# Two heads on the two partition halves for the first 64 queries of the diagonal blocks in a fused attention and channel-mix kernel

## What is computed

```python
raw = jnp.einsum('bhid,bhjd->bhij', q, k)
scores = sips_alpha[0] * jnp.tanh(raw / sips_beta[0])
scores = scores + lam * hamming[:, None, :, :]       # hamming = soft_bits @ soft_bits.T / 2
scores = scores + lat                                # hexc_i Mh hexc_j, per head
scores = jnp.where(causal[None, None], scores, -jnp.inf)
attn = jax.nn.softmax(scores, axis=-1)
out = jnp.einsum('bhij,bhjd->bhid', attn, v)
...
x = _layernorm(x + attention(x))
x = _layernorm(x + r * (k_act @ W_v.T))              # r = sigmoid(xr W_r), k_act = relu(xk W_k) ** 2
```

## Time and profile before

| | us |
|---|---|
| median of 3 runs | 400.71 |
| lowest, highest | 400.51, 401.08 |
| the profiled execution | 402.91 |
| its span in the trace | 401.2 |

### The profile page before, as it was taken

How to read it: one execution, slowest core, us unless ns; L and a number is a source line. 1 busy time by engine, 2 the same in 40 slices (tenths; PEclk the granted TensorE clock), 3 DMA queues, 4 the chain that set the end, 5 groups by cost and what they waited for, 6 DMA issues and landing times.

```text
span 401.2 us, 9042 instructions
## 1 busy us (share of the span) xinstructions
PE 361.6 (90%) x3045; PEld 209.1 (52%) x3045; DVE 333.0 (83%) x536; ACT 327.9 (82%) x367; POOL 229.8 (57%) x367
## 2 busy tenths in 40 slices
PE   7788878489999999999999999999989998989983
PEld 7473433134665565655564556455634564445572
DVE  4878979348999999989999999999978977797654
ACT  1216899538998999899999999899989998999811
POOL 4516557314578648765777567956684537344542
PEclk9999999859999999999999999999999999999998
DMA  4264786787613576357544763475337630100000
GB/s 127 72 192 144 233 235 177 205 236 174 155 59 116 159 196 176 100 157 189 154 139 128 203 158 116 146 204 159 117 116 209 174 95 2 54 26 3 2 28 26
DMA packets 37809, 53.76 MB, mean 134 GB/s; under 512 B 3523, under 2 KB 35267, under 8 KB 36191
## 3 DMA queue, kind: packets, MB, share of 16 engines
q1 hardware_dynamic: 32909, 50.83, 45.9%
q10 hardware_dynamic: 4865, 2.49, 2.5%
HBM read 38.69 MB, written 14.61 MB: 133 GB/s over the span
## 4 chain that ended last, share of the span: by engine, by line
PE 54%; DVE 12%; ACT 10%; issue 7%; DMA 6%; SPq 6%; POOL 4%; POOLq 0%; DVEq 0%; ACTq 0%
PE raw L521 25%; PE side_bank L521 13%; PE sums L521 12%; DMA i_stack<-hamming_i 5%; ACT probs L829 4%; DVE probs L1073 4%; ACT probs L834 4%; PE side_bank L613 3%; SPq L387 2%; POOL parts L975 2%; POOL res L1003 1%; DVE bn L1158 1%; DMA probs<-in_L_attn_hex_w 1%; SPq L403 1%; ACT k_act L846 1%
## 5 line engine op out<-in xcount | busy, mean ns | idle before, releaser
L1073 DVE SCALAR_TENSOR_TENSOR probs<-probs,scal,raw 128x1024 f32<-128x1024 f32 x160 | 202.3, 1273 | 35.6 <-PE raw L521 35.0
L829 ACT ACTIVATE probs<-raw 128x1024 f32<-128x1024 f32 x160 | 164.4, 1028 | 33.0 <-PE raw L521 30.6
L834 ACT ACTIVATE probs<-probs 128x1024 f32<-128x1024 f32 x160 | 169.8, 1063 | 0.3 <-DVE probs L1073 0.3
L962 POOL TENSOR_SCALAR_AFFINE_SELECT probs<-probs 128x256 f32<-128x256 f32 (+1 forms) x224 | 97.2, 450 | 114.0 <-ACT probs L834 113.6
L521 PE MATMUL raw<-i_stack,j_stack 111*128 111x384 bf16 (+3 forms) x512 | 97.8, 303 | 11.7 <-DMA i_stack<-hamming_i 7.8
L521 PE MATMUL raw<-q_stack,k_stack 72*128 72x384 bf16 (+3 forms) x512 | 97.8, 303 | 9.6 <-DVE probs L1073 7.5
L521 PE MATMUL sums<-probs,values 128*32 128x256 f32 (+2 forms) x1280 | 82.4, 384 | 0.4 <-POOL probs L962 0.4
L521 PEld LDWEIGHTS raw<-q_stack,k_stack 72*128 72x128 bf16 x512 | 42.4, 98 | 58.8 <-DVE probs L1073 27.4
L521 PEld LDWEIGHTS raw<-i_stack,j_stack 111*128 111x128 bf16 x512 | 41.4, 98 | 55.8 <-issue 22.6
L521 PEld LDWEIGHTS sums<-probs,values 128*32 128x32 f32 x1280 | 33.8, 109 | 30.2 <-issue 20.0
L975 POOL TENSOR_TENSOR parts<-whole,parts 128x512 bf16<-128x512 f32 x30 | 35.6, 1195 | 3.8 <-DVE parts L1112 3.1
(11 more groups left out here) (154 smaller groups left out, 347.8 us busy)
## 6 DMA issues: line engine op xcount, KB each, us to landing
q_stack<-q_rows SPq DMA_DIRECT2D x21, 384.0 KB
k_stack<-k_rows SPq DMA_DIRECT2D x21, 384.0 KB
i_stack<-lattice_i SPq DMA_DIRECT2D x21, 288.0 KB
i_stack<-hamming_i SPq DMA_DIRECT2D x21, 288.0 KB
q_rows<-parts SPq DMA_DIRECT2D x8, 384.0 KB, 4.3
k_rows<-parts SPq DMA_DIRECT2D x8, 384.0 KB, 2.6
k_rows<-parts SPq DMA_DIRECT2D x8, 256.0 KB, 2.9
x_res<-in_L_attn_x SPq DMA_DIRECT2D x8, 256.0 KB, 3.0
```

Of the source, the lines that this page charges most:

```text
L829: nc.scalar.activation(pair_probs(t), raw[:, t % PSUM_PAIRS, :].rearrange("p (u i) -> p u i", u=2), ACT.Tanh).then_inc(tanh_done, 1)
L834: nc.scalar.activation(pair_probs(t), pair_probs(t), ACT.Exp).then_inc(exp_done, 1)
L962: last = nc.gpsimd.affine_select(out=v, in_=v, compare_op=ALU.is_ge, fill=0.0, base=0, pattern=[[0, v.shape[1]], [1, P]], channel_multipli ...
L1073: v.scalar_tensor_tensor(out=o, in0=o, scalar=scal[:, 2:3], in1=raw[:, t % PSUM_PAIRS, :].rearrange("p (u i) -> p u i", u=2), op0=ALU.mult ...
```

## The change

Each diagonal block of 128 x 128 is cut at query 64. Its first 64 queries see only the block's first 64 keys. These 64 x 64 squares leave the ordinary pairs: the product of key block jb now starts at query 128 jb + 64 and has 448, 320, 192 or 64 columns, so a quad takes four pairs in place of five. The squares of 8 heads (four key blocks each) are put into one *square pair*, the first four heads on partitions 0 to 63, the other four on 64 to 127. A half batch (8 heads) has 8 ordinary pairs and one square pair, and a batch 18 pairs.

With it come these edits. The square pair's scores are 32 products of 64 x 64, its biases 8 of 64 x 256; a new operand `square_values` holds the two halves' values one above the other, 0 elsewhere, filled by two more copies of VectorE in `values_in`. The ordinary masks are two selects of 2 x 64 columns. The square mask is a product with `triangle`, one GpSimd instruction over 1024 elements. The `mid` parts of batches from the loop on are made by GpSimd, by subtraction, not by VectorE's cast. `PAIR_BUFFERS` is 9. All step tables are new for 18 steps. GpSimd fills the new constants in the set-up.

```diff
-PAIR_BUFFERS = 10
+PAIR_BUFFERS = 9
-VALUES_STEPS = [7, 9, 9, 9, 9, 13, 13, 14, 14, 14, 19, 19, 19, 20, 20, 23, 23, 25, 25, 25]
+VALUES_STEPS = [8, 8, 8, 8, 10, 10, 14, 14, 14, 17, 17, 17, 17, 20, 20, 23, 23, 23]
...
+            k, j = divmod(t, HALF_PAIRS)
+            quad, p = 2 * k + j // 4, j % 4
+            heads = [4 * quad + 2 * (p % 2) + u for u in range(2)]
             if p < 2:
...
+                return [[(h, 3, 0), (h, 0, SQUARE)] for h in heads]
+            return [[(h, 2, 0), (h, 1, P + SQUARE)] for h in heads]
...
+                if is_square(t):
+                    for jb in range(JB):
+                        for r in range(4):
+                            for s in range(2):
+                                first_key = square_heads(t, s)[r] * T + jb * P
+                                at = 4 * SQUARE * jb + SQUARE * r
+                                last = mm(raw[SQUARE * s:SQUARE * (s + 1), t % PSUM_PAIRS, at:at + SQUARE],
+                                          k_stack[par][:, first_key:first_key + SQUARE],
+                                          q_stack[par][:, first_key:first_key + SQUARE])
...
+                if is_square(t):
+                    for jb in range(JB):
+                        for s in range(2):
+                            heads = square_heads(t, s)
+                            at = 4 * SQUARE * jb
+                            queries = i_stack[par][:, heads[0] * T:(heads[3] + 1) * T] \
+                                .rearrange("p (r i) -> p r i", r=4)[:, :, jb * P:jb * P + SQUARE]
+                            last = mm(raw[SQUARE * s:SQUARE * (s + 1), t % PSUM_PAIRS, at:at + 4 * SQUARE],
+                                      j_stack[par][:, jb * P:jb * P + SQUARE], queries)
...
+                if is_square(t):
+                    squares = pair_probs(t).rearrange("p u i -> p (u i)")
+                    for jb in range(JB):
+                        for r in range(4):
+                            at = 4 * SQUARE * jb + SQUARE * r
+                            last = mm(sums[32 * r:32 * r + 32, jb * P:jb * P + SQUARE],
+                                      square_values[par][:, jb, 4 * k + r, :], squares[:, at:at + SQUARE],
+                                      start=False, stop=(jb == JB - 1), skip_group_check=True)
...
+                if is_square(t):
+                    v = v.rearrange("p u (n i) -> p (u n) i", i=SQUARE)
+                    nc.gpsimd.tensor_tensor(v, v, triangle[:].unsqueeze(1).broadcast_to([P, 2 * T // SQUARE, SQUARE]),
+                                            ALU.mult).then_inc(mask_done, 1)
+                    return
...
+                for s in range(2):
+                    dst = square_values[1 - parity[0]][SQUARE * s:SQUARE * (s + 1)].rearrange("p j (k r) m -> p (j k) r m", k=2)
+                    last = v.tensor_copy(dst[:, :, :, NP * s:NP * s + HD], src[0:SQUARE, :, s])
```

More of the change, by code:

```diff
@@ new lines, in weighted @@
+                first_pair = last_of_group(t) - 1
+                blocks = [[(0, SQUARE, SQUARE, 224)], [(0, SQUARE + 224, SQUARE + 224, 224), (3, 3 * P + SQUARE, 0, SQUARE)],
+                          [(1, P + SQUARE, P + SQUARE, T - P - SQUARE)], [(2, 2 * P + SQUARE, 0, P + SQUARE)]][p]
+                for n, (jb, first, at, size) in enumerate(blocks):
+                    for r in range(4):
+                        last = mm(sums[32 * r:32 * r + 32, first:first + size], values[par][:, jb, 4 * (2 * k + s) + r, :],
+                                  pair_probs(first_pair + r // 2)[:, r % 2, at:at + size],
+                                  start=(s == 0 and p == 0 and n == 0), stop=False, skip_group_check=True)
```

162 lines of the change are left out of this document (88 added, 74 removed).

## The result

| | before | after |
|---|---|---|
| median of 4 runs, us | 400.89 | 411.61 |
| lowest, highest | 400.51, 403.53 | 409.99, 414.28 |
| span of the profiled execution | 401.2 | 409.8 |
| mean granted clock of TensorE | 0.979 | 0.945 |

The ratio is 1.0259, 95% interval 1.019 to 1.0329. The change made the kernel slower, by 1.9 to 3.3%. The forecast was 389.5 us with a range of 382 to 399; the measured time lies outside that range, and on the other side of the kernel before. Ratios and their intervals leave out executions more than 1.5% above the fastest one of the same kernel, medians do not.

A forecast was written before the change was run, and what follows sets the result against it. TensorE was taken as the bound, ScalarE in batches 6 and 7. Batches 1 to 5 -7.0, batches 6 and 7 -6.8, front +0.8, tail +1.8 gave -11.2 us: 391.7 profiled, 389.5 as median; range 382 to 399.

The forecast's parts named there:

- If its 2.6 us of gaps and waits stayed ... I take 2.3 us: TensorE's gaps and waits in a steady batch: 2.3 us in place of 2.6, giving 40.6 us a batch.
- VectorE loses ... four casts of 0.60: VectorE's work a batch: two steps of 1.27 us and four casts go, two copies come, 39.6 to about 35.5.
- That room covers the 6.2 on average.: GpSimd's added 6.2 us a batch is covered by its 11 us a batch of waiting for ScalarE's exponentials.
- I priced the issue of each: TensorE's many small products: each further one takes 25 ns, so their issue is not the limit.
- The front, "+0.8": Stack loads for batch 1 land up to 0.8 us later for VectorE's two copies; GpSimd's new constants cost nothing.
- The tail, "+1.8": At the end, the last square mask adds 1.7 us on the path to the output, its products 0.1.
- forecast 0.87: A square pair's 32 score products on TensorE, with the two half-arrays loading weights side by side: 0.87 us.
- the rival of loads in series: Small weight loads on TensorE run one after another: +2.4 us a batch, 405.1 us in all; chance 0.12.
- The relief of ScalarE and VectorE: Work a batch falls on ScalarE from 39.9 to about 36.2 us, on VectorE from 39.6 to about 35.5.
- 3.4 us less than 41: Batches 6 and 7, without preparation: ScalarE bounds a period near 41 us; 3.4 us less for each.
- The likeliest case: The whole kernel's forecast of 386 to 394 us; chance 0.55.
- GpSimd sets the pace: Near a batch's end, GpSimd's parts and masks make each batch wait 1 us: 396.5 us; chance 0.15.

The follow-up runs named there:

- nine: The kernel with three edits, but the square pairs masked on TensorE by eight more products a pair, GpSimd keeping one small select; 390.61 us, ratio 0.9698.
- ten: The kernel with three edits, but the four middle parts of a batch cast by VectorE again in place of GpSimd; 415.23 us, ratio 1.0342.
- twelve: The kernel before, with only the middle parts moved from VectorE's casts to GpSimd; 401.56 us, ratio 0.9994.
- fourteen: The changed kernel with J and G rows written first, loop kept, 15 of 16 value products of each batch's first square pair left out; 402.04 us, one run.
- run thirteen: The kernel of run eleven, with GpSimd's new constants put off until VectorE's middle part of G in the set-up is cast; 384.10 us, ratio 0.9566.
- six: The kernel before, with only TensorE's loop written out; 402.28 us, ratio 0.998.
- the kernel with three edits: The changed kernel with J and G rows written first, TensorE's loop written out, and G's GpSimd parts moved behind the first norm; 386.97 us, ratio 0.9625.
- run five: The changed kernel with only TensorE's loop over batches 1 to 4 written out; 409.57 us, ratio 1.0079.
- run eleven: The kernel with three edits, with the square pairs masked on TensorE in the last batch alone; 384.91 us, ratio 0.9601.
- run seven: The changed kernel with J and G rows written ahead of Q and K, and TensorE's loop written out; 397.57 us, ratio 0.9928.

## Why the prediction was wrong

**The steps that failed, largest first.**

- *"If its 2.6 us of gaps and waits stayed ... I take 2.3 us".* This one carried the sign, and it was taken without naming what is late next. All step tables were new, so the waits could not be carried over. In the loop's four batches, waits took 15.3 us and the lower clock 6.8, for which the sum had no term. I had quoted the order's place where K's low part becomes GpSimd's last, and looked at masks and norms behind it. SyncE's queue I did not follow: J's rows stand behind K's in `write_rows`, and the next cast of J, now in step 2, behind them. Where I took 0.3 us a batch off the waits, the cast came late and beside the square mask: 2.4 us of standstill in each of three batches. The wait was to be read from code and order alone.
- *"VectorE loses ... four casts of 0.60".* The row held the hint. A cast with a mean of 602 ns takes 0.42 alone. I used the mean as the price and did not ask what stood beside the long ones. The trace of the kernel before has a small form of the collision in each steady batch (the two rows below). The changed kernel put the longest GpSimd instruction of the program, the square mask of 2.35 us, beside such a cast. The size of that mask I had right (2.35, measured 2.36).
- *"That room covers the 6.2 on average."* For the amount this held: runs nine, ten and twelve show no price on GpSimd's load. The same paragraph says what a late operation delays, and names masks only. Late was the norm, behind two parts of G: 1.4 us a batch.
- *The loop.* TensorE's instructions rose from 3,045 to 4,197 products with as many loads, and I priced the issue of each and not the turn: 2.5 us, and a clock of 0.96 in the batch. The Trainium skill has a rule for it (Runtime: NRT & Kernel Launch, section "Instruction fetch mechanics"): a taken branch whose target is no longer held forces a fetch. It puts the store of TensorE at 2,048 instructions. The direction agrees; that a body of some 2,006 records stops too (fourteen) does not fit a limit of 2,048 for the body alone.
- *The front, "+0.8".* First tanh +3.8. The fills were said to be covered by 8.48 us of GpSimd's idling. They were, on GpSimd; VectorE's cast beside them was not. With the fills put off (run thirteen) the first tanh comes at 30.6, which is +0.9 and near the 0.8 of the two copies. The load that batch 1 waits for was issued at 66.02 and landed at 84.94, 3.2 us later than before. Batches 0 and 1 took 2.0 us less, so by batch 2 the net was +1.8. That 2.0 is not a gain to rely on: the kernels of runs six and twelve, whose set-up is that of before but for the middle parts in twelve, took 93.5 us there, and the traced kernel before 96.0.
- *The tail, "+1.8".* The last mask was as forecast. Batch 7 with the tail came to -0.7 in place of -1.6, at a clock of 0.91 where before had 0.98; what the clock cost there no run separates.

**What held.** TensorE's own terms were right or cautious. The 32 square scores are followed by the next group after 0.63 us (forecast 0.87):

```profile
214.75 0.69 PE L533 MATMUL raw<-q_stack,k_stack 72*64 72x64 bf16 x32
215.38 0.61 PE L533 MATMUL raw<-i_stack,j_stack 111*128 111x192 bf16 x4
```

So the rival of loads in series is out. That the kernel came out slower all the same, which I had given to that rival, has another cause. The relief of ScalarE and VectorE came as computed: 36.8 and 36.7 us in batches 2 to 5 as a mean, 36.4 and 35.4 in the kernel with three edits, forecast 36.2 and 35.5. Batch 6 takes 37.5 us, forecast 37.6; that the two agree is in part luck, for it was forecast as 3.4 us less than 41 and came as 4.1 less than 41.6. A steady batch without the stops takes 39.6, forecast 40.6. The likeliest case was a description of the kernel with three edits (387.0 us), not of the one that was timed. The rival "GpSimd sets the pace" had the right engine and the wrong mechanism, and its price of 1 us a batch above the forecast was under a quarter of what came (180.1 against 162.9 in batches 2 to 5, 4.3 a batch).

**What could have been seen.** I gave 0.13 to slower, nearly all for one mechanism on TensorE. With every table rewritten, a wait on a queue that nobody re-sorted deserved a chance of its own, and its place could be found before the run. The collision could be found too, in the kernel before, where the cast of J stands beside a low part that GpSimd makes:

```profile
198.75 1.16 POOL L975 TENSOR_TENSOR parts<-whole,parts 128x512 bf16<-128x512 f32 x1
...
199.05 1.14 DVE L1107 CAST parts<-feats 128x512 bf16<-128x512 f32 x1
```

## What to carry to other kernels

When steps are re-ordered, follow each buffer round its whole ring: who writes it next, which DMA must have read it, and what stands ahead of that DMA in its queue. A mean duration well above the shortest one is to be looked up for a collision, which here mattered more than the load of the engine that causes it. Where one stop is taken away, look again at what now meets: run five shows a collision that the stop had kept off. Before a loop body is made longer, look at what the turn of the loop costs now, and again after.

## What the runs showed of the hardware

- VectorE's f32 to bf16 cast of 128 x 512, SBUF to SBUF, takes 0.42 us alone. Where it begins while a GpSimd instruction runs, it ends 0.2 to 0.4 us after that one has ended, in all 29 cases of the kernel before and in 23 of 24 of the changed kernel: 2.32 and 2.57 us beside the square mask, 1.37 beside a select of 64 x 1024, 1.14 beside a low part. Where it began first, by 0.36 us (183.29 and 183.65 in the changed kernel), it took 0.42. The 24th is the cast in the set-up, which two fills held too that follow the addition at once (3.07 us; GpSimd from 18.79 to 21.72). VectorE's main step reads one operand from PSUM; the 20 of them that begin beside a square mask in the changed kernel took 1.27 to 1.28 us. The Trainium skill (GPSIMD Engine Reference, section "8. Key points") says that GpSimd shares its SBUF interfaces with VectorE and contends with those of its instructions that are in a 2-port performance mode or have two SBUF inputs. The cast has one input, and no trace shows its mode; that it contends is shown, and that here it is not a slower pace but a standstill.
- A branch back of TensorE, with about 2,006 and 2,132 recorded instructions in the body, cost 3.24 and 2.46 us of standstill; with 1,557 nothing that could be seen.
- Eight products of 256 columns for biases, four on each half of the array, and as many for the mask go by in 1.0 us together (run eleven, 357.45 to 358.47 us), and 32 products of 64 x 64 on the two halves in 0.63 (214.75 to 215.38 in the changed kernel).
- Batches with a stop of 2 us and more on TensorE had stretches at the 1.2 GHz level in most cases (0.93 to 0.96 as a mean; batch 4 of the changed kernel, with a stop of 2.38, had 1.00), and batches whose longest stop was some 1.4 us had none (1.00 in batches 2 to 4 of run seven).
